# A dense stage's variance sums: three bfloat16 products of parts split on GpSimd, in place of one float32 product

## The reference

```python
h = (1.0 + eps) * x + agg
h = relu(_ln(h @ w1 + b1, g1, be1))     # 256 -> 1024
h = relu(_ln(h @ w2 + b2, g2, be2))     # 1024 -> 1024
y = h @ w3 + b3                         # 1024 -> 256
out = relu(_ln(x + y, bn_g, bn_b))
x = x + out
...
def _ln(x, g, b):
    m = mean(x, axis=-1);  v = var(x, axis=-1)
    return (x - m) * rsqrt(v + 1e-5) * g + b
```

## Time and profile before

| | |
|---|---|
| median of three runs | 3133.91 us (3132.59 to 3136.23) |
| the profiled execution | 3134.97 us |
| its span in the profile | 3133.0 us |
| mean granted TensorE clock | 0.903 |
| busy, share of the span | TensorE 78%, VectorE 71%, GpSimd 63%, ScalarE 51% |
| dense stage | from about 1130 to about 2070 us of the span |

### The profile page before, as it was taken

One profiled execution on the slowest core, in us unless ns is written; L12 is line 12 of the kernel. 1 busy time (PEld: TensorE's weight loads), 2 busy tenths in 40 slices (PEclk: granted clock), 3 DMA queues, 4 the chain that ended last, 5 costly groups with the idle time before them and its releaser, 6 DMA issues. The chain is left out here.

```text
span 3133.0 us, 88320 instructions
## 1 busy us (share of the span) xinstructions
PE 2456.0 (78%) x29338; PEld 2164.5 (69%) x29339; DVE 2233.0 (71%) x3932; ACT 1592.6 (51%) x3967; POOL 1984.4 (63%) x2094
## 2 busy tenths in 40 slices
PE   2677677777777779999999999938777777777773
PEld 2566666666666679999999999936555555555652
DVE  6566667776777657777777777758777777777777
ACT  6555555555555558888888888821111111111114
POOL 5677767777777724454544444437777777777772
PEclk9988889888899989999999999969888888988896
DMA  7555555555555510000000000026555555555554
GB/s 168 165 152 160 152 147 159 164 162 160 158 157 160 148 45 17 23 20 21 23 20 21 20 23 20 23 77 178 172 173 170 171 174 174 167 174 172 172 171 135
DMA packets 183986, 373.55 MB, mean 119 GB/s; under 512 B 42741, under 2 KB 93959, under 8 KB 183912
## 3 DMA queue, kind: packets, MB, share of 16 engines
q0 software_dynamic: 75552, 209.45, 23.7%
q1 hardware_dynamic: 107392, 162.37, 17.2%
q10 hardware_dynamic: 968, 0.87, 0.1%
HBM read 346.95 MB, written 25.80 MB: 119 GB/s over the span
## 5 line engine op out<-in xcount | busy, mean ns | idle before, releaser
L550 POOL DMA_INDIRECT rows<-tab_scratch,srcs x784 | 750.7, 958 | 264.4 <-issue 229.3
L1561 POOL DMA_INDIRECT a_rows<-tab_scratch,srcs x784 | 751.7, 959 | 250.9 <-issue 226.7
L1627 PE MATMUL sum_ps<-feat,a_hot 128*125 128x264 f32 x1960 | 599.0, 462 | 207.1 <-DVE feat L1720 98.1
L1627 PEld LDWEIGHTS sum_ps<-feat,a_hot 128*125 128x125 f32 x1960 | 417.6, 222 | 310.3 <-issue 117.8
L979 PE MATMUL z_ps<-ah,w 128*128 128x125 f16 x6400 | 555.1, 219 | 2.7 <-PEq L1075 2.6
L979 PE MATMUL z_ps<-al,w 128*128 128x125 f16 x3200 | 544.1, 218 | 0.0
L979 PEld LDWEIGHTS z_ps<-ah,w 128*128 128x128 f16 x6400 | 490.8, 97 | 3.5 <-issue 3.4
L1571 ACT ACTIVATE feat<-d 128x32 f32<-128x32 f32 x196 | 44.9, 229 | 827.2 <-DVE d L1716 580.5
L626 PE MATMUL sum_ps<-hot,rows 128*128 128x125 f16 x1960 | 356.1, 235 | 53.0 <-PEq L642 24.6
L612 PE MATMUL mlp_ps<-ewa,eab 128*128 128x256 f16 x788 | 213.9, 301 | 229.6 <-PEq L608 229.1
L626 PE MATMUL sum_ps<-hot,rh 128*128 128x125 f16 x1960 | 354.4, 234 | 0.0
(11 more groups left out here) (220 smaller groups left out, 5938.7 us busy)
## 6 DMA issues: line engine op xcount, KB each, us to landing
ea<-edge_t SPq DMA_DIRECT2D x394, 128.0 KB
dstb<-dst_flat SPq DMA_DIRECT2D x98, 512.0 KB, 4.0
rows<-tab_scratch,srcs POOLq DMA_INDIRECT x784
a_rows<-tab_scratch,srcs POOLq DMA_INDIRECT x784
tab_scratch<-prow SPq DMA_DIRECT2D x50, 128.9 KB
hx<-x SPq DMA_DIRECT2D x50, 125.0 KB
x_scratch<-x SPq DMA_DIRECT2D x50, 125.0 KB
hs<-tab_scratch SPq DMA_DIRECT2D x50, 125.0 KB
```

Of the source, the lines that this page charges most:

```text
L550: pool.indirect_dma_start(rows[:, b % DEEP, k, :], None, dram["tab0"], bass.IndirectOffsetOnAxis(ap=srcs[:, c:c + 1], axis=0),).then_inc(r ...
L1561: pool.indirect_dma_start(rows[:, b % DEEP, k, :], None, dram["tab1"], bass.IndirectOffsetOnAxis(ap=srcs[:, c:c + 1], axis=0),).then_inc(r ...
L1627: ins = pe.matmul(out[:], hot[:, h, k, :], feat[:, row, k, :], start=(k == 0), stop=(k == CB - 1))
```

## The change

Both variances get another third step. GpSimd splits the folded sum into three bfloat16 parts: it copies `ssq` into a bfloat16 tile (part 0), subtracts that from `ssq`, copies the rest (part 1), and subtracts again, which leaves part 2. These are four more instructions in each `folded`, and each of them waits for the one before; the last one signals `ssq_ready`. TensorE then makes three products of the parts with a bfloat16 matrix of 1/1024, which add up in the same place in PSUM, and the last of them signals `var_done`. A memset for that matrix stands ahead of the one for `ones`, which stays. What is computed is the same up to rounding.

```diff
         ssq = [a[j][:, 0, :] for j in (0, 1)]
+        ssq16 = [m.sb(f"ssq16_{j}", [P, 3, TN], BF16) for j in (1, 2)]
+        ones16 = m.sb("ones16", [P, P], BF16)
...
                 settled(pool.tensor_tensor(a[j][:, 0:4, :], a[j][:, 0:4, :], a[j][:, 4:8, :], ALU.add))
                 settled(pool.tensor_tensor(a[j][:, 0:2, :], a[j][:, 0:2, :], a[j][:, 2:4, :], ALU.add))
-                pool.tensor_tensor(ssq[j], a[j][:, 0, :], a[j][:, 1, :], ALU.add).then_inc(ssq_ready[j], 1)
+                settled(pool.tensor_tensor(ssq[j], a[j][:, 0, :], a[j][:, 1, :], ALU.add))
+                settled(pool.tensor_copy(ssq16[j][:, 0, :], ssq[j]))
+                settled(pool.tensor_tensor(ssq[j], ssq[j], ssq16[j][:, 0, :], ALU.subtract))
+                settled(pool.tensor_copy(ssq16[j][:, 1, :], ssq[j]))
+                pool.tensor_tensor(ssq16[j][:, 2, :], ssq[j], ssq16[j][:, 1, :], ALU.subtract).then_inc(ssq_ready[j], 1)
...
                 pe.wait_ge(v_read, 1)
                 pe.sem_inc(v_read, -1)
-                pe.matmul(v_ps[j], ones[:], ssq[j], start=True, stop=True).then_inc(var_done[j], 1)
+                for q in range(3):
+                    ins = pe.matmul(v_ps[j], ones16[:], ssq16[j][:, q, :], start=(q == 0), stop=(q == 2))
+                ins.then_inc(var_done[j], 1)
...
             low_e(0)
+            dve.memset(ones16[:], 1.0 / H)
             dve.memset(ones[:], 1.0 / H).then_inc(ones_ready, 1)
```

## The result

The changed kernel takes 3333.35 us (3324.19 to 3340.37, four runs) against 3133.25 for the kernel before beside it: ratio 1.0638, 95% interval 1.0604 to 1.0672. That is 200 us more; 3342 was predicted. The profiled execution took 3339.05 us with a span of 3336.9.

A forecast was written before the change was run, and what follows sets the result against it. A ring through GpSimd, as long as TensorE's own work, was taken to bind: 4.06 + 1.0 - 0.7 - 0.1 = 4.3 us a body, 198 over 46 bodies plus 10 outside, so 3342 us; range 3267 to 3425.

The forecast's parts named there:

- the ring: Chain from one variance(1) to the next through ScalarE, GpSimd and VectorE; four links, 18.27 us, as long as TensorE's work.
- the first link: From variance(1) to the end of folded(0), 6.70 us; forecast to grow by 1.2 us a body.
- the second link: From the end of folded(0) through VectorE to layer 2's squares, 7.26 us; claimed to bind, forecast change 0.
- The tails: Four added dependent GpSimd steps behind each fold: 2.03 us each, both counted in full, 4.06 us a body.
- The collisions: GpSimd against VectorE: a step of folded(1)'s tail held up, +1.0 us; folded(0)'s first fold freed, -0.7 us a body.
- The products: On TensorE, three products take 0.10 us less than one float32 product; counted once, through variance(1): -0.1 us a body.
- The sum: 4.06 + 1.0 - 0.7 - 0.1 = 4.3 us a body; 198 us over 46 bodies, 10 us outside them.
- the relief of the first fold: folded(0)'s first fold on GpSimd no longer runs beside VectorE's scaling: 1.25 us instead of 1.95, -0.7 a body.
- B: Rival: tails hidden, TensorE's 0.10 us counts in each variance; 10 us off, 3124 us; chance 0.02.
- A: Rival: only the tail before variance(1) pays, play takes up folded(0)'s; 1.9 us a body, 3226 us; chance 0.10.
- C: Rival: TensorE's clock falls too after its wait ahead of variance(1); 6.1 us a body, 3425 us; chance 0.15.

The follow-up runs named there:

- e8: Kernel before, with GpSimd's last fold writing the sum as float16 and one float16 product in both variances, no tail: 3129.35 us, ratio 0.9991.
- e6: Kernel before, with VectorE's wait for the scaled output rows moved behind `low_h()` and `inverse(0)`: 3167.61 us, ratio 1.0126.
- e3: Changed kernel without tails: the fold writes the sum once as bfloat16, three products read it and two zero parts: 3126.14 us, ratio 0.9980.
- e2: Changed kernel, with the split tail and three products only in the first hidden layer's variance, the other as before: 3206.29 us, ratio 1.0236.
- e1: Changed kernel, with the split tail and three products only in the second hidden layer's variance, the other as before: 3305.61 us, ratio 1.0558.
- e10: e1 plus 40 unused products ahead of TensorE's wait for the sum in variance(1), `v_read` wait moved ahead in both variances: 3253.19 us, ratio 1.0379.
- e7: Changed kernel plus 40 unused products ahead of TensorE's wait in variance(1), `v_read` wait moved ahead in both variances: 3310.63 us, ratio 1.0580.

## Why the prediction was right

**What bounds.** Right for the change, not quite for the kernel before. TensorE was busy 100 us in 100, and still a body grew by what was put on GpSimd, and giving TensorE 0.4 us a body back (e8) gave nothing. But in the kernel before the ring through GpSimd falls short of binding, at one place by 0.21 us: ahead of layer 2's squares VectorE waits for ScalarE's copy (e6), and in the first link for its own row statistics (e8). That the second link kept its length to 0.01 us was no proof: folded(0) ends 2.48 to 2.50 us behind VectorE's scaling of the second hidden layer in all 45 bodies, since that scaling holds up its first fold, and ScalarE's strand hangs on the same scaling (line 1210 starts 4.89 us behind its end). For an added tail of 2.11 us the 0.21 matters little; for a gain it is decisive.

**The tails.** Right: 2.11 us against 2.03. A cast takes 0.29 us (0.25 from the nearest rows), a subtraction 0.41 to 0.42, a gap 0.17 to 0.18. By the Trainium skill's line rate (GPSIMD Engine Reference, Engine selection) a cast would have been an estimated 0.10 us; what a one-input step of 125 columns takes here is 0.29, and the measurement decides. With the 402 ns for 264 columns that leaves some 0.19 us that does not go with the columns, an estimate from two different instructions.

**The collisions.** Right: 0.92 us a body in the tail of folded(1) against 1.0; the first fold has a mean of 1248 ns, where the earlier trace rows show 1.95 us in the one body and 1.25 for the other fold. Over both, its busy time fell from 153.8 to 124.8 us by the groups of the two pages, 0.58 a body against 0.7.

**The products.** The 0.1 us was right in size; alone it gives 6 us in all (e3).

**The second link.** Forecast 0, measured -0.12 as the mean of two cases: 6.80 where variance(0) follows folded(0) at once (15 of the 45 bodies), 7.0 to 7.3 and more where TensorE comes late. In the first case 0.21 us are the play above. The rest is that ScalarE's rows come sooner, and GpSimd's step for them no longer meets VectorE (0.73 us at 1580.02 instead of 1.45 at 1513.34; VectorE's scaling takes 1.17 us there instead of the 1.64 of the earlier trace rows). The sum had neither. In the second the clock takes it back.

**The sum.** That 4.3 came out at 4.32 is partly luck: the tails took 0.16 us a body more than forecast and the relief of the first fold was 0.12 smaller, and against that stand 0.08 from the collision and 0.12 from the second link. Outside the whole bodies the span grew by 5 us and not 10.

**The rivals.** B, faster, is out: even with no tail there are 6 us to be had. A is out by e2. C was half right: the clock falls, to 0.94 over the stage, and costs some 16 us, but the prediction had it cost little because VectorE would not be ready sooner; what covers it is folded(0)'s tail, as e1 shows, where that cover is gone and the clock takes some 40. The wait ahead of variance(1), 2.6 to 3.7 us in the 45 bodies, is shorter than the 3.9 that C started from, in part since slow products take some of it.

**What stays open.** Why the fall of the clock doesn't come in every body was not settled. In the 45 bodies all 15 with a lag of 0.3 us follow a wait of 2.6 to 2.9 us ahead of variance(1), but so do 12 of the other 30. And whether a shorter strand of ScalarE and VectorE would make the kernel before faster was not tried.

## What to carry to other kernels

An engine that is busy 100% may still have no say in the pace: follow one tile from a wait to the same wait of the next tile. A link that keeps its length to a hundredth of a microsecond need not bind, as both its ends may hang on one earlier step; what binds shows where the waiting instruction starts a fixed short time behind the end of one thing it needs, body after body. Four small steps of 0.29 to 0.42 us that wait for each other cost 2.1 us, here to save 0.1, and a half-used engine is no cover if the next engine waits for its last step. Halves of a change add up only where nothing else fills the gap: one tail alone cost 174 us, and both 200, because a slow clock ran beside the second.

## What the runs showed that was not expected

- Adding 40 useless products a body, with the wait moved ahead of them, made two kernels faster, by some 53 us (e10 against e1) and 23 us (e7 against the change); 7 and 8 of that are the moved wait's. The granted clock of the stage went from 0.91 (e1) and 0.94 (the change) to 1.00 in both.
- With one wait less between the sum's signal and the true products, they started 0.14 us behind the end of the last step on GpSimd instead of 0.30, at variance(0) too, where no product was added (e7).
- A kernel whose clock falls in some bodies scatters: e1's four executions lie 54 us apart, those of e2, at full clock, 5.
